# Second attention's score stage: ScalarE's squares and cosine parts stand ahead of LayerNorm rows, GpSimd's coefficients ahead of value parts

## The reference

```python
x = x + proj(softmax(q k / 16) v)            # q, k, v of group_norm(x), 8 groups
t = tokens(x)                                # (1024, 256)
xn = ln(t) / (norm(ln(t)) + 1e-12)           # second attention
t = t + softmax((xn xn^T) ** 2) @ ln(t)
y = clip(ln(t) @ (sign(w - mean(w)) * mean(abs(w))) + b, -1, 1)
t = t + round(7 y) / 7
```

## Time and profile before

| | us |
|---|---|
| median of 3 runs | 1812.44 (1809.83 to 1814.81) |
| the profiled execution's own time | 1809.89 |
| its span | 1808.2 |
| PE busy in it | 1745.4 (97%) |
| DVE busy | 1372.9 (76%) |
| ACT busy | 941.5 (52%) |
| POOL busy | 732.1 (40%) |

### The profile page before, as it was taken

How to read it: one execution, slowest core, us unless ns; L and a number is a source line. 1 busy time by engine, 2 the same in 40 slices (tenths; PEclk the granted TensorE clock), 3 DMA queues, 4 the chain that set the end, 5 groups by cost and what they waited for, 6 DMA issues and landing times.

```text
span 1808.2 us, 34770 instructions
## 1 busy us (share of the span) xinstructions
PE 1745.4 (97%) x11938; PEld 1604.0 (89%) x11938; DVE 1372.9 (76%) x2580; ACT 941.5 (52%) x1476; POOL 732.1 (40%) x1334
## 2 busy tenths in 40 slices
PE   7899999999999999999999999999999999999997
PEld 6898888988889988899888999889998888998887
DVE  6678777787777877778787777877778777787675
ACT  3545646455463654735547354564645546455462
POOL 0442616326162361614526144261542616336161
PEclk9999999999999999999999999999999999999999
DMA  3404124050330504205041140412404023050320
GB/s 117 126 24 152 36 81 128 23 169 17 104 105 23 186 0 127 82 35 174 0 150 59 58 151 7 154 48 72 137 23 155 31 93 116 23 186 1 96 91 24
DMA packets 97055, 152.88 MB, mean 85 GB/s; under 512 B 11648, under 2 KB 70400, under 8 KB 97024
## 3 DMA queue, kind: packets, MB, share of 16 engines
q1 hardware_dynamic: 97024, 152.48, 26.5%
HBM read 76.95 MB, written 75.50 MB: 84 GB/s over the span
## 4 chain that ended last, share of the span: by engine, by line
PE 53%; POOL 14%; issue 11%; ACT 7%; DMA 6%; DVE 6%; SPq 1%; POOLq 1%; DVEq 0%; ACTq 0%
PE wide L373 19%; PE narrow L373 5%; PE wide L475 3%; PE narrow L475 3%; PE wide L477 3%; PE narrow L477 3%; PE wide L476 3%; PE narrow L476 3%; DMA e_back<-e_scratch 3%; PE turn L584 3%; DMA e_scratch<-x_norm 3%; PE turn L545 2%; ACT expo L749 2%; POOL ln_r L1278 2%; POOL val L1304 2%
## 5 line engine op out<-in xcount | busy, mean ns | idle before, releaser
L373 PE MATMUL wide<-xn_hi,prob 128*128 128x512 f32 x1024 | 303.5, 398 | 0.0
L787 ACT ACTIVATE ln<-tok,ln_shift,ln_r 128x256 f32<-128x256 f32 x128 | 68.4, 593 | 297.8 <-POOL ln_shift L1280 297.8
L373 PEld LDWEIGHTS wide<-xn_hi,prob 128*128 128x128 f32 x1024 | 185.5, 188 | 38.2
L1275 POOL TENSOR_TENSOR ln_v<-ln_mv,ln_eps 128x2 f32<-128x2 f32 (+2 forms) x128 | 26.7, 208 | 471.0 <-DVE ln_mv L1081 240.8
L756 ACT ACTIVATE prob<-e_back 128x1024 fp32r<-128x1024 f32 x112 | 118.3, 1056 | 141.8 <-DMA e_back<-e_scratch 141.7
L1322 POOL TENSOR_TENSOR carrier_p<-ones 128x1 f32<-128x1 f32 x60 | 11.6, 193 | 437.0 <-DVE y_sb L1091 434.5
L749 ACT ACTIVATE expo<-wide,neg_max 128x1024 f32<-128x1024 f32 x128 | 142.4, 1113 | 70.7 <-DVE neg_max L1011 70.1
L1018 DVE STREAM_TRANSPOSE x_norm<-expo 128x1024 f32<-128x1024 f32 x112 | 139.1, 1242 | 45.1 <-ACT expo L749 44.8
L1011 DVE TENSOR_REDUCE neg_max<-wide 128x1 f32<-128x1024 f32 x128 | 155.6, 1215 | 15.8 <-PE wide L373 15.3
L373 PE MATMUL wide<-xn_lo,prob 128*128 128x512 f32 x512 | 160.8, 395 | 0.0
L1023 DVE TENSOR_TENSOR prob<-e_back,prob 128x1024 fp32r<-128x1024 f32 x112 | 135.9, 1214 | 31.2 <-ACT prob L756 31.2
(11 more groups left out here) (179 smaller groups left out, 5525.2 us busy)
## 6 DMA issues: line engine op xcount, KB each, us to landing
e_scratch<-x_norm SPq DMA_DIRECT2D x112, 512.0 KB, 3.0
e_back<-e_scratch SPq DMA_DIRECT2D x448, 128.0 KB, 3.1
x_raw<-in_x SPq DMA_DIRECT2D x32, 512.0 KB, 4.0
out<-y_sb SPq DMA_DIRECT2D x32, 512.0 KB, 3.6
tok<-in_L_conv_qkv_w SPq DMA_DIRECT2D x1, 768.0 KB, 6.8
ln<-in_L_conv_proj_w SPq DMA_DIRECT2D x1, 256.0 KB, 6.8
ln<-in_L_ffn_weight SPq DMA_DIRECT2D x1, 256.0 KB, 3.3
out_bias<-in_L_conv_proj_b SPq DMA_DIRECT2D x1, 128.0 KB, 3.6
```

The lines of the kernel that those rows point to most:

```text
L373: mm = pe.matmul(o, lhsT, r, start=first and i == 0, stop=last and i == len(parts) - 1)
L787: act.activation(ln2[:, n], tok[:, n], ACT.Identity, bias=ln2_shift[:, n:n + 1], scale=ln2_r[:, n:n + 1]).then_inc(ln2_made, 1)
```

## The change

On ACT, in `front`, between `unit_rows(b, 1)` and `exp2(b, 5)`: the hi cosine part of group 1 goes ahead of the LayerNorm rows of group 2; `exp2(2)` and the cosine part of group 2 go ahead of the LayerNorm rows of group 3; the cosine part of group 3 goes ahead of the LayerNorm rows of group 4, and `exp2(4)` ahead of the unit rows of group 4. On POOL the coefficients of group 4 go ahead of the value part of group 2, and `e2_lo(2)` ahead of the value part of group 3. No instruction, operand, semaphore or buffer is added or removed. PE, DVE and SP issue in the order they had.

```diff
@@ -862,18 +862,18 @@
                 exp2(b, 1)
                 layer_norm1(b, 1)
                 unit_rows(b, 1)
+                cosT_hi(b, 1)
                 layer_norm1(b, 2)
-                cosT_hi(b, 1)
                 unit_rows(b, 2)
+                exp2(b, 2)
+                cosT_hi(b, 2)
                 layer_norm1(b, 3)
-                cosT_hi(b, 2)
-                exp2(b, 2)
                 unit_rows(b, 3)
                 exp2(b, 3)
+                cosT_hi(b, 3)
                 layer_norm1(b, 4)
+                exp2(b, 4)
                 unit_rows(b, 4)
-                cosT_hi(b, 3)
-                exp2(b, 4)
                 cosT_hi(b, 4)
                 exp2(b, 5)
                 exp2(b, 6)
@@ -1349,11 +1349,11 @@
                 value_lo(b, 1)
                 layer_norm1(b, 3)
                 lengths(b, 3)
-                value_lo(b, 2)
                 layer_norm1(b, 4)
                 lengths(b, 4)
+                value_lo(b, 2)
+                e2_lo(b, 2)
                 value_lo(b, 3)
-                e2_lo(b, 2)
                 e2_lo(b, 3)
                 value_lo(b, 4)
                 e2_lo(b, 4)
```

## The result

The changed kernel takes 1796.37 us (median of 4 runs, 1794.72 to 1798.97), the kernel before 1811.13 (4 runs, 1809.58 to 1814.81): a ratio of 0.9917 with a 95% interval of 0.9896 to 0.9937, so 0.8% faster. The profiled execution took 1795.91 us; 1795.7 had been forecast.

A forecast was written before the change was run, and what follows sets the result against it. PE, busy 97%, was taken as the bound: 2.33 us idle per image less 0.46 returned gives 1.87, cut by POOL's lo weights to 0.89; sixteen images give 14.2, so 1809.89 - 14.2 = 1795.7 us, range 1788 to 1811.

The forecast's parts named there:

- The ceiling: PE's idle time inside an image, three waits in the second score stage: 2.33 us per image, 37 us (2.1%) in all.
- ScalarE's moves: ACT's new order shortens PE's three score-stage waits: 2.33 less 0.46 that returns, so 1.87 us per image.
- The first wait: PE's wait before scores2(2) for tokT_lo of group 1: all 0.70 us was to go.
- what returns: New PE waits in the score stage, for tokT_lo(2) (0.3 to 0.4 us) and before turn_e2(4) (0.1 or 0.2): 0.46 us.
- the second: PE's wait before turn_e2(2) for ACT's exponential of part 2: the 0.62 us was to go.
- the third: PE's wait before turn_e2(4) for ACT's exponential of part 4: 1.01 us was to shrink to 0.1 or 0.2.
- POOL's chain decides: POOL's lo weights for product2(0)'s tiles 6 and 7 limit the gain to 0.89 us per image, not 1.87.
- The order of the turns: DVE and POOL: whichever waits longer goes first; e2_lo(6), 0.12 behind e2_hi(7), ends at 878.5, e2_last_lo(7) at 879.2.
- The rule against the row: On DVE's and POOL's shared port, a row charged POOL 0.15 us per cast; the skill's rule says the loser fully blocks.
- rival 1: Every DVE cast costs POOL its full time (0.35, 0.42, about 0.55): no gain, 1811 us; chance 0.16.
- Rival 2: PE keeps all it gets in the score stage, 1.87 x 16 = 30 us: 1780 us; chance 0.06.
- Rival 3: On POOL xn_lo gets in ahead of e2_last_lo(7), tile 7 2.3 us late: slower, 1844 us; chance 0.09.

The follow-up runs named there:

- e4_interleaved: Changed kernel, with PE doing tiles 0 to 5 of product2(0) and product2(1) before tiles 6 and 7 of both; 1778.65 us, ratio 0.9825.
- experiments 3: Changed kernel with e2_lo(6) made over 128 of its 896 columns, the rest of tile 6's lo weights left out; 1778.55 us, ratio 0.9828.
- 10: Changed kernel with ScalarE's hi cosine part of group 1 put back behind the LayerNorm rows of group 2; 1796.97 us, ratio 0.9933.
- Experiment 8: e8_turn6_first: changed kernel with VectorE's e2T_parts(6) moved ahead of e2_hi(7) and e2_last_lo(7); 1808.32 us, ratio 0.9999.
- e2_pool_only: Kernel before with only the GpSimd part of the change, ScalarE's order as before; 1798.47 us, ratio 0.9939.
- e7_inter_pool: Kernel before with only the GpSimd part of the change, plus PE's tiles 0 to 5 of product2(0) and product2(1) first; 1791.88 us, ratio 0.9903.

## Why the prediction was right

- *The ceiling, 2.33 us per image.* `e4_interleaved` reached 1.92 of it (110.72 less 108.80).
- *ScalarE's moves.* The lead at `scores2(7)` was put at 1.87; it is 1.71 in this image and 1.89 in the mean. The first wait went whole (0.87 with what is drawn as busy). Of what returns, the wait for `tokT_lo(2)` was there (`scores2(4)` 0.50 behind transposes that take 0.25). For the wait before `turn_e2(3)`, 0.37 in this image, the sum has no term. The one before `turn_e2(4)`, which I had at 0.1 to 0.2, is not drawn, but at the pace that the products ahead of these transposes had before, they would start at 861.85 and not at 861.96, so 0.11 is there. The old waits in their turn had cost more than the view draws: PE's lead rises by 0.87 at the first (0.70 drawn), by 0.78 at the second (0.62) and by some 1.12 at the third (1.01), 2.77 in place of 2.33. So by this estimate some 1.06 returned, not 0.46. The two errors offset each other, and that part of the agreement is luck.
- *POOL's chain decides.* Right, by experiments 3, 4 and 10: PE's lead over 0.7 to 0.9 or so per image is waited off. The end of `e2_lo(6)` was put at 878.5 and came at 879.02 on the old clock. Three terms were too small. The chain began 0.22 late (860.23 for 860.01), since ACT waited 0.2 longer for the DMA of `e_back` in this image; in the mean of 14 images it began 0.02 late, so "moves forward by as much" failed in this image only. A turn of DVE costs POOL 0.25 and 0.23 (one-tile value parts 0.99 and 0.97 for 0.74), where I charged 0.15 and 0.22. And the casts of parts 2 and 3 cost the coefficients 0.27 in all (`len_e` 0.35 for 0.19, `len_x` 0.30 for 0.19), where I charged 0.06.
- *The order of the turns.* As forecast: copy of part 7, `e2_lo(6)` with 0.12 more (2.23 for 2.12), then `e2_last_lo(7)`. It ended at 879.57 for 879.2 forecast.
- *What the profile would show.* L373 and L545 fell as forecast. L475 was put at 12 to 20 us, released by POOL and DVE; 10.5 is drawn, all of it by POOL, and the wait for DVE before tile 7 (0.08 by the starts) is drawn as busy. The mean of the casts L1055 was to rise and fell, from 853 to 729 ns: it is the subtraction L1060 that waits now, 2559 ns for 1663.
- *The sum.* 0.89 per image was forecast and 0.78 measured, 12.5 us. The total met 14.2 by 1.5 us of the first 100 us that are no part of the change: the forecast time is closer to the measured one than its steps are.
- *The rule against the row.* A turn costs POOL 0.23 to 0.25, where the copies' own time is 0.35 to 0.42 by the rows of before; I charged 0.15 and 0.22. With the copies' full time, rival 1, the forecast would have been 1811, no gain. The Trainium skill, "SBUF — State Buffer", section "SBUF: two separate sides", says that the loser fully blocks for the whole instruction. This trace agrees that DVE and POOL take turns, but the turn costs POOL less than the copy's whole time, and the measurement decides.
- *The rivals.* Rival 2 (PE keeps all) did not happen, and experiment 4 shows what it would have been (1778.65 for 1780). Rival 3 (`xn_lo` first) did not happen in the changed kernel: `xn_lo` starts at 872.30, 0.35 after the subtraction got its turn (872.64 less 0.69), for which it had waited since 870.15. Experiment 8 shows what it costs.

What stays open: why runs of one half differ by up to 5.7 us (1794.63 to 1800.31 for `e2_pool_only`), since only the fastest of these five has a trace.

## What to carry to other kernels

When waits of the bounding engine are removed, look for the next thing that it needs behind them and how long before use that was ready (0.33 us here): this cover, and what the producer of that thing gets earlier itself (0.62 here, by the order of two engines' turns), is the gain, and not the waits. GpSimd, which has next to no gaps here, got only 0.15 earlier by being reordered. Where the producer can't get earlier, let the consumer come later, by putting other work of it in between. And judge each move alone and with the limit lifted: here either half brings three quarters of the gain by its median, and one of the moves brings none that can be measured.

## What the runs showed of the hardware

- Two engines at one gate with 0.06 us between them cost 2.2 us or nothing: `xn_lo` at 103.64 against the subtraction at 103.70, and 878.69 against 878.68. The order is settled by hundredths of a microsecond and differs from image to image in one execution. Both times the loser ended its own time, less 0.13 to 0.16 us, after the other's end: the subtraction 0.56 after `xn_lo` (0.69 alone), `xn_lo` 2.25 after the subtraction (2.41 alone).
- Where both engines wait, the one that has waited longer went first in every row looked at, and each turn of a copy cost POOL 0.11 to 0.25 us.
- PE's busy time in the page rose by 9.4 us with the same instructions, since waits of 0.1 to 0.25 us are drawn as busy. PE's idle time (span less busy) fell by 23.4 us, from 62.8 to 39.4, and the span by 14.0.
- A wait of PE of 2.54 us in `product2(0)` is followed by a granted clock of 0.50 in `e8_turn6_first` (107 to 110), and one of 2.56 likewise (0.63 over 1652 to 1656). In the eleven other traces the clock stays at 1.00 from 20 us on until a wait of PE of 2.4 us at L584 near the end (1796.2 in the trace of before); the longest wait of PE in between is 1.51 (`e7_inter_pool`).
